# Four layers on one core: layer 1 as one program over four samples, and layer 3's expert numbers packed eight to a load

## What is computed

```python
for layer in (0, 1, 2, 3):
    xn = _layernorm(x)
    s = attn[layer](xn)
    g = _silu(ffn[layer](xn))
    x = x + s * g

def _L1_attn_ref(inputs, Wq, Wk, Wvdown, Wvup):
    score = jnp.einsum('bqd,bkd->bqk', inputs @ Wq, inputs @ Wk) / jnp.sqrt(32.)
    score = jnp.where(causal, score, 0.0)
    score = jnp.where(score != 0, score, NEG_FILL)
    return jax.nn.softmax(score, axis=-1) @ (inputs @ (Wvdown @ Wvup))

def _L1_ffn_ref(x, router_w, router_b, expert_w, expert_b):      # 8 experts, the best one
    probs = jax.nn.softmax(xt @ router_w + router_b, axis=-1)
    out_all = jnp.einsum('th,ehd->ted', xt, expert_w) + expert_b[None]
    return gate[:, None] * out_all[argmax]

def _L3_ffn_ref(x, router_w, w_fc, w_proj, shared_fc, shared_proj):   # 8 experts, the best two
    out = sum(_mlp(flat, w_fc[e], w_proj[e]) * combine[:, e:e + 1] for e in range(E))
    return out + _mlp(flat, shared_fc, shared_proj)
```

## Time and profile before

| what | value |
|---|---|
| median of 3 runs | 1582.71 us (1582.23 to 1583.55) |
| the profiled execution | 1592.05 us, span 1588.6 us, mean granted PE clock 0.89 |
| busy share PE / PEld / DVE / ACT / POOL | 79% / 53% / 65% / 47% / 38% |
| layer 1, its four calls | 657.4 us to 841.9 us of the span |
| layer 3's tile steps | 1408.6 us to 1563.8 us |

### The profile page before, as it was taken

How to read it: one execution, slowest core, us unless ns; L and a number is a source line. 1 busy time by engine, 2 the same in 40 slices (tenths; PEclk the granted TensorE clock), 3 DMA queues, 4 the chain that set the end, 5 groups by cost and what they waited for, 6 DMA issues and landing times. The chain is left out here.

```text
span 1588.6 us, 21351 instructions
## 1 busy us (share of the span) xinstructions
PE 1247.1 (79%) x7092; PEld 839.1 (53%) x7092; DVE 1031.5 (65%) x2384; ACT 739.7 (47%) x1565; POOL 606.7 (38%) x601
## 2 busy tenths in 40 slices
PE   0799999998997877366767697888787874988985
PEld 0345565564554566255555364655555553766664
DVE  0367667768787535256653798898899896524444
ACT  0345555555544325133323768567668571443322
POOL 1243344344328713323310153553533444135551
PEclk9989999999999788578867899898999897799998
DMA  7300000000000022421000000000000000001113
GB/s 166 93 0 2 1 1 1 1 2 1 1 1 24 32 64 82 146 84 49 14 1 11 0 1 1 1 0 1 1 1 1 0 1 15 13 21 34 34 32 91
DMA packets 54456, 40.72 MB, mean 26 GB/s; under 512 B 13191, under 2 KB 46701, under 8 KB 54349
## 3 DMA queue, kind: packets, MB, share of 16 engines
q1 hardware_dynamic: 35660, 24.30, 5.2%
q0 software_dynamic: 4544, 9.32, 2.1%
q10 hardware_dynamic: 14146, 5.75, 1.7%
HBM read 26.32 MB, written 13.04 MB: 25 GB/s over the span
## 5 line engine op out<-in xcount | busy, mean ns | idle before, releaser
L762 POOL TENSOR_TENSOR PR<-PR,R 128x256 f32<-128x256 f32 (+3 forms) x128 | 160.9, 1258 | 269.5 <-DVE R L1216 264.6
L1692 POOL TENSOR_TENSOR YY<-YY,H 128x512 f32<-128x512 f32 x120 | 162.2, 1374 | 209.0 <-DVE H L2063 208.8
L2055 DVE TENSOR_TENSOR_SCAN H<-DA,H 128x1024 f32<-128x1024 f32 x64 | 164.7, 2574 | 0.2
L415 PEld LDWEIGHTS banks<-we,HH 128*128 128x128 f32 x1024 | 144.8, 205 | 37.0 <-issue 32.3
L1033 ACT ACTIVATE PR<-banks,NM 128x129 f32<-128x129 f32 (+3 forms) x256 | 132.4, 526 | 44.7 <-DVE NM L1193 43.8
L415 PE MATMUL banks<-XT,we 128*128 128x512 f32 x256 | 138.1, 658 | 11.1 <-ACT HH L1910 11.1
L415 PE MATMUL banks<-we,HH 128*128 128x128 f32 x1024 | 144.9, 288 | 0.0
L415 PE MATMUL banks<-BCR,SEL 96*128 96x512 f32 x128 | 67.8, 531 | 75.7 <-DVE H L2063 64.3
L1910 ACT ACTIVATE HH<-banks,be1f 128x512 f32<-128x512 f32 x128 | 83.8, 686 | 91.9 <-PE banks L415 91.1
L415 PEld LDWEIGHTS banks<-PTS,V 128*64 128x64 f32 x1280 | 73.0, 144 | 99.9 <-issue 91.4
L415 PE MATMUL banks<-PTS,V 128*64 128x128 f32 x1280 | 105.3, 296 | 16.3 <-DVE PTS L1201 10.0
(11 more groups left out here) (532 smaller groups left out, 2571.9 us busy)
## 6 DMA issues: line engine op xcount, KB each, us to landing
xsort<-zrow SPq DMA_DIRECT2D x1, 3072.0 KB, 13.1
XS<-xsort SPq DMA_DIRECT2D x12, 256.0 KB, 2.9
ysort<-PTS SPq DMA_DIRECT2D x12, 256.0 KB, 2.2
pj_stage<-in_L_ffn_w_proj SPq DMA_DIRECT2D x1, 2048.0 KB, 9.9
we<-in_L_ffn_we SPq DMA_DIRECT2D x1, 2048.0 KB, 10.6
we<-yrows SPq DMA_DIRECT2D x8, 256.0 KB, 4.8
X<-in_L_attn_resid_pre ACTq DMA_DIRECT2D x4, 256.0 KB, 4.6
xrows<-XN SPq DMA_DIRECT2D x4, 256.0 KB, 2.3
```

Source lines behind the costliest of these rows:

```text
L415: return nc.tensor.matmul(o, l, r, start=start, stop=stop)
L762: nc.gpsimd.tensor_tensor(p, p, R[:, n, :].unsqueeze(2).to_broadcast([P, 2, w]), ALU.mult).then_inc(pn, 1)
L1692: nc.gpsimd.tensor_tensor(YY[:, m, :], YY[:, m, :] if n else XD[m], H[:, k % 4, m, :], ALU.add).then_inc(ya, 1)
L2055: nc.vector.tensor_tensor_scan(h, DA[:, k % 4, :, :].rearrange("p m s -> p (m s)"), h, 0.0, ALU.mult, ALU.add).then_inc(scn, 1)
```

## The change

`layer1` takes no sample any more. It is one block with one barrier at its end, of B + 1 = 5 steps. Step j has the front of sample j (normalising, queries, keys, logits, scores, masks, maxima, exponentials, choice of the expert) and the back of sample b = j - 1 (weights, eight experts, transposed probabilities, values, silu, output), written between each other on each engine. What both halves need at once is doubled (`XT`, `V`, `SC`, `L`, `R`, `WG2`), the probabilities stay in `SC`, `FI` and `PT` shrink to two tiles each, and the scores use banks 6 and 7 only, the transposed probabilities and values 4 and 5. POOL gathers the next sample's rows ahead of its four adds. SP issues all weight loads of layers 3 and 2 at the block's start.

In layer 3 DVE packs eight expert numbers into one integer (each is a digit to base 8); PE loads one integer for eight tiles and gets each number by a shift and a mask in registers.

```diff
-        def layer1(b):
-            X = X4[:, b, :, :]
+        def layer1():
...
+                    @block.sync
+                    def _(sp):
+                        load_layer3(sp, *weights3)
+                        load_layer2(sp)
...
-                        if b + 1 < B:
-                            gather_rows(g, b + 1, YG, yg)
+                        for j in range(B):
+                            g.wait_ge(var, j + 1)
+                            norm_pool(plink, mv[:, :, 1], rstd[:, :]).then_inc(rs, 1)
+                            if j + 1 < B:
+                                if j:
+                                    g.wait_ge(ya, j)
+                                gather_rows(g, j + 1, YG, s_back[j + 1])
+                            for t in range(T):
+                                g.wait_ge(fi, T * j + t + 1)
+                                nc.gpsimd.tensor_tensor(SC[:, j % 2, t, :], SC[:, j % 2, t, :], FI[:, t % 2, :], ALU.add).then_inc(fd, 1)
...
+                        for j in range(B + 1):
+                            b = j - 1
+                            front, back, more = j < B, j > 0, j + 1 < B
...
+                        def weights(b):
+                            pe.wait_ge(wgs, b + 1)
+                            if b + 1 < B:
+                                pe.wait_ge(ya, b + 1)
...
+                        def store_bias(b):
+                            act.wait_ge(bi, b + 1)
+                            if b:
+                                act.wait_ge(gt, b)
+                            nc.scalar.activation(ACC[:, :, :].rearrange(flat), PS[:, 0, :], ACT.Copy).then_inc(bis, 1)
...
+                        def add_expert(b, e):
+                            n = NE * b + e
+                            v.wait_ge(yp, n + 1)
+                            if e:
+                                v.wait_ge(ad, n)
+                            else:
+                                v.wait_ge(bis, b + 1)
...
-                                e = nc.tensor.value_load(TEI[0:1, i:i + 1], min_val=0, max_val=E - 1)
+                                if i % 8 == 0:
+                                    packed.append(nc.tensor.value_load(TEI[0:1, i // 8:i // 8 + 1], min_val=0, max_val=E ** 8 - 1))
+                                e = (packed[i // 8] >> (3 * (i % 8))) & (E - 1)
...
+                        for i in range(8):
+                            nc.vector.memset(radix[:, i:i + 1], float(E ** i))
+                        nc.vector.memset(TEF[:, NS:8 * NG], 0.0)
...
-                        link(nc.vector.reduce_sum(TEF[:, 0, :], TE[:, :, :], AX.X))
-                        nc.vector.tensor_scalar(TEI[:, :], TEF[:, 0, :], float(E - 1), None, ALU.min)
+                        link(nc.vector.reduce_sum(TEF[:, 0:NS], TE[:, :, :], AX.X))
+                        link(nc.vector.tensor_scalar(TEF[:, 0:NS], TEF[:, 0:NS], float(E - 1), None, ALU.min))
+                        digits = TEF[:, :].rearrange("o (g i) -> o g i", i=8)
+                        link(nc.vector.tensor_tensor(digits, digits, radix[:, :].unsqueeze(1).to_broadcast([1, NG, 8]), ALU.mult))
+                        link(nc.vector.reduce_sum(TEG[:, :], digits, AX.X))
+                        nc.vector.tensor_copy(TEI[:, :], TEG[:, :])
...
-        for b in range(B):
-            layer1(b)
-            end_stage()
+        layer1()
+        end_stage()
```

More of the change, by code:

```diff
@@ L1469, in transposes, with values @@
                             last.then_inc(tr, 1)
[L1471 to L1472 removed]
+                        def values(b, t):
+                            pe.wait_ge(pt, T * b + t + 1)
                             for kt in range(T):
[L1474 removed]
+                                last = mm(PS[:, 4 + t % 2, 0:P], PT[:, t % 2, kt * P:(kt + 1) * P], V[:, b % 2, kt, :],
@@ new lines, in gate_next @@
+                        def gate_next(b):
+                            act.wait_ge(ya, b)
+                            nc.scalar.activation(YC[:, :, :], YC[:, :, :], ACT.Silu).then_inc(gn, 1)
+                        for j in range(B + 1):
+                            b = j - 1
+                            front, back, more = j < B, j > 0, j + 1 < B
+                            if back:
+                                store_weights(b)
+                                store_pt(b, 0)
+                                store_bias(b)
+                                store_pt(b, 1)
+                            if front:
+                                turned(j)
+                            if back:
+                                store_s(b, 0)
+                                store_s(b, 1)
+                            if front:
+                                store_qk(j)
+                            if back:
+                                store_pt(b, 2)
+                                store_pt(b, 3)
+                            if front:
+                                router(j)
+                            if back:
+                                store_s(b, 2)
+                                store_s(b, 3)
+                            if front:
+                                store_v(j)
+                                exps(j, 0)
+                                exps(j, 1)
+                            if more:
+                                store_choices(j + 1)
+                            if front:
+                                exps(j, 2)
+                                exps(j, 3)
+                            if back:
+                                gate(b)
+                            if more:
+                                gate_next(j + 1)
@@ L2498, in final @@
                             last.then_inc(fo, 1)
-                        experts = []
+                        experts, packed = [], []
                         to_features(0)
```

401 lines of the change are left out of this document (255 added, 146 removed).

## The result

| | before | after |
|---|---|---|
| median (us) | 1583.02 (1582.23 to 1583.55, 4 runs) | 1533.09 (1526.52 to 1542.43, 4 runs) |
| ratio of after to before, 95% interval | | 0.9689 [0.9632, 0.9747] |
| profiled execution: time, span | 1592.05, 1588.6 | 1542.43, 1540.7 |

The change takes about 50 us off; 46 were forecast. The profiled execution is the slowest of the four of after; its span is 47.9 us shorter than the one before. Both profiled executions are 9.3 us slower than the median of their kernel (the one before against its first three runs, 1582.71). The four runs lie 1% apart, and the longer ones have the lower mean granted clock: 1526.5 at 0.904, 1528.8 at 0.902, 1537.4 at 0.894, 1542.4 at 0.892.

What follows compares the result with a forecast made beforehand. The prediction took layer 1 to be bound by its chain of waits and layer 3's tiles by PE's path. Savings of 35.0 and 10.95 us, 46.0 in sum, gave 1536.7 us from 1582.71, range 1522 to 1557.

Steps and rivals of the forecast that it cites:

- What bounds the kernel: Layer 1's calls are bound by their chain of waits, not by an engine; layer 3's tiles by PE's path.
- Layer 1: Five steps with waits along DVE's queue, plus 2.1 us for the clock: 149.5 us, 35.0 less than 184.5.
- Expert 2: ... Wait 1.0: Full paired step of layer 1: DVE waits 1.0 us for PE's transposes, values and expert 2 after normalising.
- the walk: Layer 1 followed along DVE's queue, wait by wait, with PE groups at the higher clock: steps sum to 147.4 us.
- DVE busy for more than 70%: Sign in layer 1: DVE busy for more than 70% of its 145 to 155 us.
- Layer 3: Fewer expert number loads save 12.0 us, packing costs 0.7 and memsets 0.35: 10.95 us less, between 6.3 and 16.7.
- the lower bound: Layer 3's loads: 0.15 us taken off for each of 31 pairs of new register instructions, leaving 7.3 us gained.
- the 1.05: Layer 3: cost in us of DVE's packing instructions and the memsets at the layer's start.
- Late rows: Sample 1's gathers in layer 1 behind weight loads: likely cost nothing; rival 7 us once, 1543.7 us, chance 0.05.
- POOL beside DVE: Gathers beside DVE's normalising in layer 1: nothing counted; rival has them exclude each other, 11.6 us, 1548.3, chance 0.06.
- The slower rival: PE never leaves 1.2 GHz in layer 1, which takes 24.5 us more than before: 1596.3 us, chance 0.04.
- The rival of the lasting lower clock: Lower PE clock lasts into half of each paired step of layer 1, which gains 22.5 us: 1549.3 us, chance 0.13.

Runs made afterwards that it cites:

- with the clock at 0.95: Changed kernel with 24 extra matmuls on PE ahead of each step's weights in layer 1, so PE isn't idle there: 1550.70 us, ratio 0.9778.
- another order: Changed kernel with experts 0, 1 and first transposes ahead of the weights, expert 2 behind the biases, two ACT calls moved: 1526.07 us, ratio 0.9653.
- the first comparison: The measurement under The result: changed kernel against the kernel before, 1533.09 against 1583.02 us, ratio 0.9689.
- the second: The changed kernel, unaltered, run again on another chip against the kernel before: 1542.51 against 1581.05 us, ratio 0.9764.
- Two of the moves: Changed kernel with only experts 0, 1 and first transposes ahead of the weights, 1540.61 us; with only expert 2 behind the biases, 1548.08 us.
- groups 1 and 3: Two sets of four follow-up kernels, each set on one chip with the kernel before, which took 1585.77 and 1586.55 us there.
- group 2: Four follow-up kernels on another chip, the unaltered changed kernel among them; the kernel before took 1581.05 us there.
- the edit that was to break up the row of transfers: Changed kernel with POOL's gather and scatter of each round's fifth tile in layer 3 issued ahead of its wait for the norms: 1548.34 us, ratio 0.9779.

## Why the prediction was right, and where it was off

**What bounds the kernel: right.** The seams and DVE's waits were the gain. The second call took 47.5 us from its statistics to the next ones, with DVE busy for 27.3; step 2 takes 36.6 with DVE busy for 26.4. So 10 of its 10.9 us less are idle time, and 0.9 are DVE's work, for which the forecast had the old 27.5.

**Layer 1: 31.9 less, not 35.0.** Of the steps, 28.0 / 37.4 / 34.6 / 30.3 / 17.1 were forecast and 28.2 / 38.9 / 36.6 / 31.0 / 17.9 measured. The row of step 1 is over the 38 us at which I had called the forecast wrong; the step of the argument that failed is "Expert 2: ... Wait 1.0". It was 2.5, 3.2 and 2.3 us. That is 5.0 us too little in three steps, where the forecast had 2.1 for all that the lower clock costs. I had PE at the higher clock from the biases on; in step 2 it fell a second time, behind PE's wait of 1.9 us for `XN`, which the walk had not looked at as an idle stretch of PE. In step 2 the first values and expert 2 ran at 1.2 GHz (0.52 in the stretch above). By the two durations of the earlier trace rows that is some 1.6 us more than at 2.4, an estimate, and most of the 2.2 by which that wait was over. What made up for a part of it is luck: DVE's own work is some 1 us less a paired step than the 27.5 I took. Of the rest, the wait for the biases in step 1 was 3.9 (2.8 forecast), the logits 2.3, 2.8 and 2.3 (2.3), the two silus 1.2 (1.3), and PE's wait for the weighing 17.6 us in three steps (6 each). "DVE busy for more than 70%" was 67%.

**Layer 3: 14.4 less, not 10.95.** The tiles gave 15.3, not 12.0: the term was too small, since PEld's idle time ahead of `fcT` (20.0 to 6.0) is nearer to the truth than PE's (13.5 to 2.8), and the new register instructions, for which the lower bound took off 0.15 each, fit into what is left of the delay, 0.16 to 0.59 us in the tiles without a load. I had also read the 0.86 us of one tile as if 35 tiles had it; two in five had about half of it or less. The packing's chain delayed the first gather by 0.7 us (it starts 55.8 us into the layer before, 56.5 after), inside the 1.05. The other 1.5 us ahead of the tiles go with the clock, 0.78 for 0.80, and the part behind the tiles took 1.3 less. The two errors, 3.1 us too much and 3.4 too little, cancel: that the sum came within 4 us of the median is luck in part.

**Late rows: nothing, right.** With both layers' weights on the way the DMA engines are full for the first 28 us:

```profile
659.50:687.50 28.00, 18.51 (x62) 11.79 (x63) 16.30 (x60) 10.13 (x18) 13.94 (x15) 0.62 1.04 329
```

and the weighing of sample 1 did not wait: it started at 681.27, 6 us before these loads ended, and step 0 took 28.16 us. That agrees with the rule of the Trainium skill ("DMA: Bandwidth & Descriptors", Queues, rings and completion order) that each DMA engine takes turns between its queues.

**POOL beside DVE: nearly nothing.** The normalising beside the gathers takes 1.34, 1.10 and 1.32 us in steps 0 to 2 (the last is the row at 727.40) instead of 1.11: 0.2 twice, where the rival had 3.9 three times. The Trainium skill's rule ("SBUF - State Buffer", Who interferes with whom), that the two exclude each other for a whole instruction, agrees where POOL computes. A fill mask takes 0.43 us alone and 0.99 to 1.00 when it starts some 0.55 us into a POOL add, ending 0.3 behind the add; ten of the 16 masks were held up by an add before and three are after, and their mean went from 751 to 535 ns. That part of the gain the forecast did not have.

**The slower rival: refuted.** PE was back at 2.4 GHz for a part of every paired step, with a mean clock of 0.77 to 0.88.

**The rival of the lasting lower clock** is where the truth leaned, by a quarter of its distance. But its reason isn't settled by the clock alone: with the clock at 0.95 step 2 stayed as long to within 0.6 us, and with another order step 1 fell by 6.9 us and step 2 by 3.9, at a clock of 0.93 and 0.87.

**Open.** Why the first comparison gave 49.9 us and the second 38.5. The spread of the runs of after goes with the mean clock, and the table shows a place of it: the head of layer 3, unchanged but for the packing, takes from 64.2 us at a mean clock of 0.86 to 72.6 at 0.75. What sets it there wasn't tried.

## What to carry to other kernels

When two programs are put into one another, list for each queue what stands behind a wait for the engine that is fed: here expert 2 behind the features, and the experts behind the weights. Work that is ready belongs in front of such waits, not only where it is needed; moving four calls by a few places gave another 16.4 us on a chip where the whole change had given 38.5, 13.8 of them in the layer that was edited. Two of the moves, tried one by one, gave 5.7 us and about nothing by layer 1's length, but on other chips; that such moves are worth more together than their sum is a guess from this and not shown.

## What the runs showed of the hardware that was not expected

- Chips seem to differ in kind and not only in speed. On the chips of groups 1 and 3 PE's products were taken up about 2 us late when POOL issued its row transfers (indirect DMAs) 0.3 us behind one another: 1.86 to 2.09 us behind the start of a transfer in layer 3's tiles in most cases, and in layer 1 mostly 2.4 to 2.8 behind the start of the last of eight gathers or of one before it. With packed numbers and one load in eight tiles, the tiles take 138.8 to 141.0 us there, and 131.6 to 131.8 in the first comparison and, where POOL's order was left alone, in group 2. That the transfers cause it is only argued, from these distances, which say little in layer 1, where a gather starts every 1.25 us; the edit that was to break up the row of transfers ran on a chip without the effect.
- The granted clock fell twice within 13 us, each time behind an idle stretch of PE: it was 0.51 (717.5 to 723.5) behind an idle stretch of 6.1 us that ended at 719.7, back at 1.00, and 0.52 (726.5 to 732.5) behind one of only 1.9 us that ended at 727.9.
- Loads of a register on PE's sequencer one behind another take 0.65 us each, though the load is recorded with 0.30 and the register instruction behind it with 0.15.
